# Step sizes of a selective scan from factored quadratics, and low rank experts with spaced gates, in a twelve-sublayer decoder

## Chip, core and metric

The program runs on one NeuronCore of one Trainium2 chip. It is one launch of 31,707 instructions. The metric is the device time of that launch in microseconds (us); of the kernel before three runs were timed.

## What is computed

A decoder of four layers on x of 8 x 128 tokens by 256 features; each layer has an attention-like part, a cross attention and a feed-forward part, and every one of the twelve is followed by a residual addition and a layernorm. The two sublayers that the change touches stand one behind the other, as third and fourth:

```python
def _L0_ffn_ref(x, Wr, br, Wd, bd, Wu, bu):          # E = 8 experts, R = 16, K = 2
    logits = jnp.einsum('btd,de->bte', x, Wr) + br
    gates = jax.nn.softmax(logits + bonus, axis=-1)
    topk_vals, topk_idx = jax.lax.top_k(gates, K)
    topk_vals = topk_vals / topk_vals.sum(axis=-1, keepdims=True)
    w = (jax.nn.one_hot(topk_idx, E, dtype=x.dtype) * topk_vals[..., None]).sum(axis=-2)
    h = jax.nn.relu(jnp.einsum('btd,edr->betr', x, Wd) + bd[None, :, None, :])
    eo = jnp.einsum('betr,erd->betd', h, Wu) + bu[None, :, None, :]
    return jnp.einsum('bte,betd->btd', w, eo)

def _L1_attn_ref(x, W_x, W_dt, b_dt, A_log, D):      # 16 states, rank 64
    dt_x, Bm, Cm = jnp.split(x @ W_x.T, [R, R + N], axis=-1)
    dt = jax.nn.softplus(dt_x @ W_dt.T + b_dt)
    dA = jnp.exp(jnp.einsum('bld,dn->bldn', dt, -jnp.exp(A_log)))
    dBx = jnp.einsum('bld,bln,bld->bldn', dt, Bm, x)
    # h = dA_t * h + dBx_t ; y_t = sum_n h * C_t, over the 128 steps
    return ys.swapaxes(0, 1) + x * D
x = _layernorm(x + _L0_ffn_ref(...)); x = _layernorm(x + _L1_attn_ref(...))
```

## The kernel before

Everything is float32 with tokens of one batch entry on 128 partitions: X is [128, b, 256], its transpose XT [128, c, 1024] with two halves c of the features. Each sublayer is one or more blocks; all engines meet at a block's end, and inside a block each engine runs its own list in the order written, tied to the others by counted semaphores (the names in `p.s`). PSUM has eight banks of 512 columns. The weights of the next sublayer are fetched by SyncE's queue during the present one.

**Low rank experts** (`low_rank_experts`). TensorE computes the router's logits in bank 0 and the hidden values of all experts in banks 1 and 2. VectorE makes the softmax of 8 gates for each token, ranks each gate against the others (L2370 "greater", L2371 "equal", for each of the 8 batch entries, then L2374 to L2376 over all), keeps the two best and scales them (L2380). TensorE turns the gates, eight pieces of 8 columns, into gatesT [8, 1024] (L2336, copied by ScalarE at L2348). VectorE adds the bias to the hidden values and multiplies the rectified ones by their gates (L2384, L2387); TensorE turns them (L2340), ScalarE copies them to hT (L2350).

**The epilogue** (`epilogue`, a helper that most sublayers share). Four rounds j of two batch entries: TensorE writes the sublayer's result for round j into bank j (`products`) and counts up y_ready; VectorE adds it to X (L525), takes statistics (L527, L530) and normalises the even entry (L536 to L539), one round behind; ScalarE does the square root and the odd entry (L504, L509). From round 2 on TensorE also turns the finished X of the round two before (L474) and ScalarE copies it to XT (L414). The experts give epilogue a function y of their own: for each batch entry one product of hT with wu (128 rows, L2392) and one of gatesT with the biases bu (8 rows, L2393), so the two kinds alternate. A float32 product shows as two passes in the trace.

**The selective scan** (`selective_scan`), first block. TensorE projects XT to the rank 64 input of the step sizes (L2574), to B and C (L2578), and the former by w_dt to the raw step sizes in banks 4 to 7 (L2583), then starts the result in banks 0 to 3 (L2591), for which GpSimd prepares selector and read. VectorE splits B and C into three bfloat16 parts (L2617 to L2624). Then it computes dt = softplus(raw + b_dt) = max(v, 0) + u * P(u), with u = exp(-|v|) and P of degree 9 for log(1 + u) / u: the bias (L2627), -|v| (L2766), the exponential by ScalarE (L2760), one scaling and nine Horner steps, each (dt + coefficient) * u, over 128x2048 (L2776, L2778), max and addition (L2779), the product with x (L2630) and a memset in decay (L2632). Each Horner step waits for the one before. The second block is the loop over the 16 states: decays by ScalarE, products by GpSimd, scans and readings by VectorE.

## Time and profile before

| what | us |
|---|---|
| median of three runs (1999.32 to 2001.83) | 1999.76 |
| the profiled execution: device time | 2003.11 |
| its span (first to last instruction) | 2001.3 |
| TensorE busy, with weight loads apart (80% of the span) | 1604.5 |
| VectorE busy (72%) | 1437.1 |
| ScalarE busy (39%) | 777.8 |
| GpSimd busy (26%) | 522.6 |
| low rank experts: first product to the last copy of XT | 731.6 to 776.0 |
| selective scan's first block | 776.3 to 825.2 |
| its loop | 825.5 to 977 |

Busy shares are means over twelve stages with different limits, so they say where an engine works, not where the time is set. The times of the last three lines are positions on the trace's clock. PEclk is the TensorE clock that was granted, as a share of its full 2.4 GHz: 0.50 is 1.2 GHz, and the mean over the span is 0.87. "Idle before" in a row is the time for which the engine did nothing ahead of the instruction; behind the arrow stands what ended it.

### The profile page before, as it was taken

To read this page: it belongs to the slowest core of one execution; us is meant where nothing else is said; L and a number is where in the kernel's file an instruction comes from. 1 tells how busy PE (TensorE), PEld (TensorE's weight loads), DVE (VectorE), ACT (ScalarE), POOL (GpSimd) and SP (SyncE) were. 2 spreads that over 40 slices of the span, in tenths; PEclk is the share of its full clock that TensorE was granted. 3 is DMA by queue.
4 is the path that set the end of the run, shared out by engine and by line. 5 is a ranking of instruction groups with operands and counts; after the bars stand their busy time and mean duration, and the time that the engine had idled before them with its cause. 6 is when DMAs were issued, how large, how long until landed. Compare 5 with 4: busy or idle time off the path is not lost. (4 is left out here: it accounts for less than half of the span.)

```text
span 2001.3 us, 31707 instructions
## 1 busy us (share of the span) xinstructions
PE 1604.5 (80%) x11439; PEld 1193.9 (60%) x11470; DVE 1437.1 (72%) x2398; ACT 777.8 (39%) x1231; POOL 522.6 (26%) x588
## 2 busy tenths in 40 slices
PE   4899999999868987266748568899995997888863
PEld 4678888887854663022446434588774885645631
DVE  3299999998645844899578573556774995657698
ACT  2367777675231532233324321433342002425532
POOL 1233333332412401377213002310000330414200
PEclk8999999999977986587878768999996998798985
DMA  3000000000000000000100001000001220010000
GB/s 143 23 28 29 26 26 26 26 26 1 1 11 13 2 7 34 0 0 0 45 3 2 27 37 72 2 25 11 12 21 42 74 73 27 4 56 2 2 0 21
DMA packets 17854, 49.20 MB, mean 25 GB/s; under 512 B 2003, under 2 KB 8276, under 8 KB 16470
## 3 DMA queue, kind: packets, MB, share of 16 engines
q1 hardware_dynamic: 17750, 47.78, 7.0%
q8 instruction: 69, 1.13, 0.2%
q14 instruction: 35, 0.29, 0.0%
HBM read 46.73 MB, written 1.05 MB: 24 GB/s over the span
## 5 line engine op out<-in xcount | busy, mean ns | idle before, releaser
L2146 DVE SCALAR_TENSOR_TENSOR arena<-psum,arena 128x1016 f32<-128x1016 f32 (+2 forms) x240 | 303.6, 1265 | 35.8 <-ACT arena L2083 30.1
L883 DVE TENSOR_REDUCE limits<-psum 128x4 f32<-128x512 f32 (+2 forms) x256 | 148.3, 620 | 91.9 <-PE psum L743 56.7
L1992 PE MATMUL psum<-ssm_XT_hi,ssm_split 128*128 128x512 f32 x640 | 195.1, 407 | 11.2 <-POOL ssm_split L1951 5.5
L851 ACT ACTIVATE PT<-psum 128x1024 f32<-128x1024 f32 x112 | 108.6, 1022 | 122.2 <-PE psum L774 122.2
L743 PE MATMUL psum<-K,QR 32*128 32x256 f32 (+1 forms) x320 | 125.1, 476 | 27.3 <-POOL K L719 16.5
L1992 PEld LDWEIGHTS psum<-ssm_XT_hi,ssm_split 128*128 128x128 f32 x640 | 116.3, 191 | 36.6 <-POOL ssm_split L1951 10.4
L2083 ACT ACTIVATE arena<-psum,arena 128x1024 f32<-128x1024 f32 x80 | 89.2, 1115 | 106.1 <-PE psum L1992 104.7
L2511 PE MATMUL psum<-expert,x 128*128 128x256 f16 x1024 | 114.2, 276 | 16.6 <-POOL expert L2497 16.6
L2649 POOL TENSOR_TENSOR fed<-dtx,b_all 128x1024 f32<-128x1024 f32 x32 | 103.2, 3245 | 77.8 <-ACT b_all L2698 44.4
L2511 PEld LDWEIGHTS psum<-expert,x 128*128 128x128 f16 x1024 | 101.3, 99 | 29.4 <-issue 16.7
L2524 DVE SCALAR_TENSOR_TENSOR acc<-psum,gate_now,acc 128x256 f32<-128x256 f32 x256 | 111.2, 483 | 8.5 <-PE psum L2511 7.7
L1950 POOL TENSOR_TENSOR ssm_split<-arena,const 128x256 fp32r<-128x256 f32 x80 | 58.5, 731 | 198.7 <-PE psum L1992 196.1
L2718 DVE TENSOR_TENSOR_SCAN state<-decay,fed 128x1024 f32<-128x1024 f32 x32 | 103.1, 3261 | 6.8 <-POOL fed L2649 5.2
L1992 PE MATMUL psum<-ssm_XT_lo,ssm_split 128*128 128x512 f32 x320 | 100.9, 397 | 0.0
L743 PEld LDWEIGHTS psum<-K,QR 32*128 32x128 f32 x320 | 60.8, 219 | 59.3 <-DVE limits L883 22.3
L2662 PE MATMUL psum<-bc_parts,selector 96*128 96x512 bf16 x64 | 23.1, 496 | 86.7 <-DVE read L2726 53.3
L2496 POOL COPY gate_now<-gates 128x8 f32 x32 | 6.1, 191 | 299.5 <-DMA expert_mask<-in_expert_masks 230.8
L762 PE MATMUL psum<-Q,KT 32*128 32x256 f32 (+1 forms) x640 | 82.9, 562 | 0.4
L1305 ACT ACTIVATE probs_g<-psum,negmax_g 128x128 f32<-128x128 f32 x128 | 45.3, 366 | 86.2 <-PE psum L1262 58.8
L498 ACT ACT_TABLE_LOAD x12 | 15.4, 1283 | 156.8 <-PEq L2528 135.3
L625 PE MATMUL psum<-XT,arena 128*128 128x512 f32 x128 | 65.0, 673 | 12.9 <-PEq L911 10.0
L790 PE MATMUL psum<-PT,V 128*32 128x128 f32 x2048 | 73.3, 291 | 2.6 <-DVE O L877 2.6
(435 smaller groups left out, 3828.4 us busy)
## 6 DMA issues: line engine op xcount, KB each, us to landing
expert_mask<-in_expert_masks SPq DMA_DIRECT2D x32, 256.0 KB, 2.6
arena<-in_ssm_in SPq DMA_DIRECT2D x16, 384.0 KB, 2.9
arena<-in_L_xattn SPq DMA_DIRECT2D x1, 5120.0 KB, 16.0
arena<-in_ssm_in SPq DMA_DIRECT2D x16, 256.0 KB, 3.0
arena<-in_L_ffn SPq DMA_DIRECT2D x1, 2592.0 KB, 10.1
arena<-in_L_xattn SPq DMA_DIRECT2D x2, 1280.0 KB, 7.8
arena<-in_L_attn SPq DMA_DIRECT2D x1, 2272.0 KB
arena<-in_L_ffn SPq DMA_DIRECT2D x1, 2176.0 KB, 8.2
```

Of the source, the lines that this page charges most:

```text
L743: ins = nc.tensor.matmul(score_bank(r)[:, k * n:(k + 1) * n], QR[group(r), b % 2, c0 + k, :], K1[group(r), b % 2, c0 + k, :, :].rearrange( ...
L762: nc.tensor.matmul(exponents[r][:, k * n:(k + 1) * n], KT[group(r), c0 + k, b * P:(b + 1) * P], Q1[group(r), b % 2, c0 + k, :, :].rearrang ...
L790: ins = nc.tensor.matmul(raw_bank(k)[group(r), slot * P:(slot + 1) * P], V[:, b, at:at + 32], PT[:, u % 2, r, slot, :], start=True, stop=True)
L851: nc.scalar.activation(PT[:, u % 2, 2 * k:2 * k + 2, :, :].rearrange("p r h q -> p (r h q)"), p.psum[:, (2 + 2 * k) * 512:(4 + 2 * k) * 51 ...
L883: ins = nc.vector.tensor_reduce(limits[:, u % 2, r, :, k], score_bank(r)[:, :].rearrange("p (h k) -> p h k", h=4)[:, :, lo:hi], AX.X, ALU. ...
L1992: ins = nc.tensor.matmul(bank[tile_bank(r, tile) + half][:, :], w_part(tile, kw, c), x_part(kx, c, slice(half * 512, (half + 1) * 512)), s ...
L2083: nc.scalar.activation(conv[:, (r + tile) % 2, :], tile_psum(r, tile), ACT.Copy, scale=tap_now[:, r, tile, TAPS - 1:TAPS]).then_inc(s.tap_ ...
L2146: ins = nc.vector.scalar_tensor_tensor(out[:, :, ago:], product[:, :, :P - ago], tap, out[:, :, ago:], ALU.mult, ALU.add)
L2511: ins = nc.tensor.matmul(bank[b][:, :D], x16[:, part, c, b * P:(b + 1) * P], expert[:, r % 2, c, :], start=(part == 0 and c == 0), stop=(p ...
L2524: nc.vector.scalar_tensor_tensor(acc[:, b, :], bank[b][:, :D], gate[:, r % 2, b:b + 1], acc[:, b, :], ALU.mult, ALU.add).then_inc(s.produc ...
L2649: nc.gpsimd.tensor_tensor(fed[:, c, :], dtx[:, c, :], b_all[:, r, :], ALU.mult).then_inc(s.input_ready.up(trips), 1)
L2718: nc.vector.tensor_tensor_scan(state[:, c, :], decay[:, c, :], fed[:, c, :], 0.0, ALU.mult, ALU.add).then_inc(s.state_ready.up(trips), 1)
```

## The change

In the low rank experts the comparisons are made for all batch entries at once. The scaled gates are also written into `gates_spaced`, [128, 2, 4, 32], where batch entry 2j + k takes the first 8 of 32 columns of group j in half k; GpSimd has cleared the rest. Two transposes then give gatesT [128, 2, 128], in which round j's gates lie on partitions 32j to 32j + 7, and bu is laid out in memory four times, on the same partitions. The function y now fills two rounds at a time: at even j four hidden products (both rounds), the bias products (j, 0), (j+1, 0) and (j, 1); at odd j the last one, (j, 1). Each bias product uses 32 rows of the array, 32j to 32j + 31.

In the scan the polynomial is written as product of four quadratics (u + a)^2 + b and one linear factor. ScalarE computes u = exp(-|raw + b_dt|) from PSUM, the squares, the linear factor and max(raw + b_dt, 0); VectorE multiplies: dt = (square + b) * dt. All of it goes by the two halves c, and two buffers of `factor` for each half let ScalarE run ahead of VectorE. The shifts a are five memsets by GpSimd.

```diff
-                for b in range(B):
-                    ins = nc.tensor.transpose(bank[3 + b // 4][:E, b % 4 * P:(b % 4 + 1) * P], gates[:, b, :], p.c("ident"))
+                for half in range(2):
+                    ins = nc.tensor.transpose(bank[3][:, half * P:(half + 1) * P], spaced[:, half, :, :].rearrange("p j e -> p (j e)"),
+                                              p.c("ident"))
...
-                for b in range(B):
-                    other = gates[:, b, :].rearrange("p (o e) -> p o e", o=1).broadcast_to([P, E, E])
-                    own = gates[:, b, :].rearrange("p (e o) -> p e o", o=1).broadcast_to([P, E, E])
-                    nc.vector.tensor_tensor(above[:, b, :, :], other, own, ALU.is_gt)
-                    ins = nc.vector.tensor_tensor(same[:, b, :, :], other, own, ALU.is_equal)
-                then(ins)
+                other = gates[:, :, :].rearrange("p b (o e) -> p b o e", o=1).broadcast_to([P, B, E, E])
+                own = gates[:, :, :].rearrange("p b (e o) -> p b e o", o=1).broadcast_to([P, B, E, E])
+                nc.vector.tensor_tensor(above[:, :, :, :], other, own, ALU.is_gt)
+                then(nc.vector.tensor_tensor(same[:, :, :, :], other, own, ALU.is_equal))
...
-                nc.vector.tensor_tensor(gates[:, :, :], gates[:, :, :], over_last(small[:, :]), ALU.mult
+                dve.wait_ge(s.operands_ready.sem, s.operands_ready.at(0))
+                pairs = lambda a: a.rearrange("p (j k) e -> p j k e", k=2)
+                nc.vector.tensor_tensor(spaced[:, :, :, :E].rearrange("p k j e -> p j k e"), pairs(gates[:, :, :]), pairs(over_last(small[:, :])), ALU.mult
                                         ).then_inc(s.gates_ready.up(), 1)
+                then(nc.vector.tensor_tensor(gates[:, :, :], gates[:, :, :], over_last(small[:, :]), ALU.mult))
...
-        def y(b, dst):
-            nc.tensor.matmul(dst, hT[:, b, :], p.w("wu"), start=True, stop=False)
-            return nc.tensor.matmul(dst, gatesT[:, b * P:(b + 1) * P], p.w("bu")[:E, :], start=False, stop=True)
+        def y(j, bank):
+            def hidden(j, k):
+                nc.tensor.matmul(bank[j][:, k * D:(k + 1) * D], hT[:, 2 * j + k, :], p.w("wu"), start=(k == 0), stop=False)
+
+            def biases(j, k):
+                group = slice(32 * j, 32 * j + 32)
+                return nc.tensor.matmul(bank[j][:, k * D:(k + 1) * D], gatesT[group, k, :], p.w("bu")[group, :], start=False, stop=(k == 1))
+
+            if j % 2:
+                return biases(j, 1)
+            for n in range(4):
+                hidden(j + n // 2, n % 2)
+            biases(j, 0)
+            biases(j + 1, 0)
+            return biases(j, 1)
...
             @block.gpsimd
             def _(pool):
+                for k, v in enumerate([a for a, _ in quadratics] + [offset]):
+                    ins = nc.gpsimd.memset(shifts[:, k:k + 1], v)
+                ins.then_inc(s.terms_ready.up(), 1)
...
-                softplus_act(p, act, state[:, :, :])
-                nc.scalar.preload_act_table(ACT.Exp)
+                act.wait_ge(s.tile_ready.sem, s.tile_ready.at(2))
+                act.wait_ge(s.terms_ready.sem, s.terms_ready.at(0))
+                raw = lambda c: p.psum[:, (4 + 2 * c) * 512:(6 + 2 * c) * 512]
+
+                def next_factor(c, k):
+                    if k >= 2:
+                        act.wait_ge(s.term_product.sem, s.term_product.at(2 * (k - 2) + c))
+                    dst, shift = factor[:, c, k % 2, :], shifts[:, k:k + 1]
+                    if k < Q:
+                        ins = nc.scalar.activation(dst, state[:, c, :], ACT.Square, bias=shift)
+                    else:
+                        ins = nc.scalar.activation(dst, state[:, c, :], ACT.Identity, scale=slope, bias=shift)
+                    ins.then_inc(s.factor_ready.up(), 1)
+
+                for c in range(DC):
+                    then(nc.scalar.activation(state[:, c, :], raw(c), ACT.Abs, bias=p.w("b_dt")[:, c:c + 1]))
+                    then(nc.scalar.activation(state[:, c, :], state[:, c, :], ACT.Exp, scale=-1.0))
+                    next_factor(c, 0)
+                for k in range(1, Q + 1):
+                    for c in range(DC):
+                        next_factor(c, k)
+                    if k == 2:
+                        for c in range(DC):
+                            nc.scalar.activation(xy[:, c, :], raw(c), ACT.Relu, bias=p.w("b_dt")[:, c:c + 1]).then_inc(s.relu_ready.up(), 1)
...
-                dve.wait_ge(s.tile_ready.sem, s.tile_ready.at(2))
+                for k in range(Q + 1):
+                    for c in range(DC):
+                        dve.wait_ge(s.factor_ready.sem, s.factor_ready.at(DC * k + c))
+                        if k:
+                            dve.wait_ge(s.term_product.sem, s.term_product.at(DC * (k - 1) + c))
+                        by = state[:, c, :] if k == 0 else dt[:, c, :]
+                        if k < Q:
+                            ins = nc.vector.scalar_tensor_tensor(dt[:, c, :], factor[:, c, k % 2, :], quadratics[k][1], by, ALU.add, ALU.mult)
+                        else:
+                            ins = nc.vector.tensor_tensor(dt[:, c, :], factor[:, c, k % 2, :], by, ALU.mult)
+                        ins.then_inc(s.term_product.up(), 1)
                 for c in range(DC):
-                    ins = nc.vector.tensor_scalar(xy[:, c, :], p.psum[:, (4 + 2 * c) * 512:(6 + 2 * c) * 512], p.w("b_dt")[:, c:c + 1], None, ALU.add)
-                then(ins)
-                softplus_dve(p, dve, dt[:, :, :], xy[:, :, :], state[:, :, :])
-                then(nc.vector.tensor_tensor(dtx[:, :, :], dt[:, :, :], p.XT[:, :, :], ALU.mult))
+                    dve.wait_ge(s.relu_ready.sem, s.relu_ready.at(c))
+                    dve.wait_ge(s.term_product.sem, s.term_product.at(DC * Q + c))
+                    then(nc.vector.tensor_tensor(dt[:, c, :], dt[:, c, :], xy[:, c, :], ALU.add))
+                    nc.vector.tensor_tensor(dtx[:, c, :], dt[:, c, :], p.XT[:, c, :], ALU.mult)
```

`quadratics` holds the four pairs (a, b) from the complex roots of the fitted polynomial, Q is 4, and the fifth factor comes from its one real root, with the leading coefficient in it.

Three places, by the order of instructions on one engine. First TensorE in the experts' epilogue, before (hT_experts are the hidden products, gatesT the biases; X are transposes):

```order
L2392 MATMUL psum<-arena,hT_experts 128x256
L2393 MATMUL psum<-arena,gatesT 128x256
L2392 MATMUL psum<-arena,hT_experts 128x256
L2393 MATMUL psum<-arena,gatesT 128x256
L2392 MATMUL psum<-arena,hT_experts 128x256
L2393 MATMUL psum<-arena,gatesT 128x256
L474 MATMUL psum<-const,X 128x128 x4
L2392 MATMUL psum<-arena,hT_experts 128x256
L2393 MATMUL psum<-arena,gatesT 128x256
L2392 MATMUL psum<-arena,hT_experts 128x256
L2393 MATMUL psum<-arena,gatesT 128x256
L474 MATMUL psum<-const,X 128x128 x12
```

and after the change, from the block's first product on:

```order
L2403 MATMUL psum<-arena,hT_experts 128x256 x4
L2407 MATMUL psum<-arena,gatesT 128x256 x4
L2403 MATMUL psum<-arena,hT_experts 128x256 x4
L2407 MATMUL psum<-arena,gatesT 128x256 x3
L478 MATMUL psum<-const,X 128x128 x4
L2407 MATMUL psum<-arena,gatesT 128x256
L478 MATMUL psum<-const,X 128x128 x12
```

The alternation of hidden and bias products becomes runs of four, and of the second run of biases the last one, that of j = 3, stands behind the first transposes.

Second, ScalarE in the first block of the scan, before:

```order
L2605 COPY dt_in<-psum 64x1024
L2606 ACT_TABLE_LOAD
L2606 ACTIVATE a<-arena 128x32
L2607 ACTIVATE a<-a 128x32
L2760 ACTIVATE state<-state 128x2048
L2609 ACT_TABLE_LOAD
```

and now:

```order
L2634 COPY dt_in<-psum 64x1024
L2635 ACT_TABLE_LOAD
L2635 ACTIVATE a<-arena 128x32
L2636 ACTIVATE a<-a 128x32
L2652 ACTIVATE state<-psum,arena 128x1024
L2653 ACTIVATE state<-state 128x1024
L2646 ACTIVATE factor<-state,shifts 128x1024
L2652 ACTIVATE state<-psum,arena 128x1024
L2653 ACTIVATE state<-state 128x1024
L2646 ACTIVATE factor<-state,shifts 128x1024 x5
L2660 ACTIVATE xy<-psum,arena 128x1024 x2
L2646 ACTIVATE factor<-state,shifts 128x1024 x2
L2648 ACTIVATE factor<-state,shifts 128x1024 x2
```

One exponential over 128x2048 and a second table load were there; now sixteen operations on 128x1024, Abs at L2652, Exp at L2653, Square at L2646, Relu at L2660 and the linear factor at L2648, behind one table load.

Third, VectorE in the same block from the last part of B and C on, before:

```order
L2624 CAST bc_parts<-bc_rest 32x1024
L2627 TENSOR_SCALAR xy<-psum,arena 128x1024 x2
L2766 SCALAR_TENSOR_TENSOR state<-xy 128x2048
L2776 TENSOR_SCALAR dt<-state 128x2048
L2778 SCALAR_TENSOR_TENSOR dt<-dt,state 128x2048 x9
L2779 SCALAR_TENSOR_TENSOR dt<-xy,dt 128x2048
L2630 TENSOR_TENSOR dtx<-dt,XT 128x2048
L2632 MEMSET decay 128x16
```

and now:

```order
L2675 CAST bc_parts<-bc_rest 32x1024
L2683 SCALAR_TENSOR_TENSOR dt<-factor,state 128x1024 x2
L2683 SCALAR_TENSOR_TENSOR dt<-factor,dt 128x1024 x6
L2685 TENSOR_TENSOR dt<-factor,dt 128x1024 x2
L2690 TENSOR_TENSOR dt<-dt,xy 128x1024
L2691 TENSOR_TENSOR dtx<-dt,XT 128x1024
L2690 TENSOR_TENSOR dt<-dt,xy 128x1024
L2691 TENSOR_TENSOR dtx<-dt,XT 128x1024
L2693 MEMSET decay 128x16
```

The bias, -|v|, the scaling and the Horner steps on full width are gone from VectorE; ten products, two additions and two products with x on half the width stand there.

## Rows read from the trace of the kernel before

**Rows 1.** Table of stretches: us, busy PE, PEld, DVE, ACT, POOL, then PEclk, DMA share, GB/s

```profile
751.70:776.20 24.50, 22.20 (x48) 10.86 (x48) 8.93 (x32) 6.72 (x13) 0.00 (x0) 0.50 0.00 0
...
791.40:825.20 33.80, 1.13 (x3) 0.19 (x1) 31.26 (x16) 3.19 (x2) 0.00 (x0) 0.58 0.00 0
825.20:977.00 151.80, 96.80 (x200) 38.03 (x200) 138.99 (x64) 52.45 (x48) 103.17 (x32) 0.80 0.00 0
```

**Rows 2.** Timeline before the scan loop: start, length, engine, line, operation, [idle before <-releaser]

```profile
779.85 3.60 POOL L2598 TENSOR_TENSOR read<-XT,arena 128x2048 f32<-128x2048 f32 x1
...
785.20 3.70 PE L2583 MATMUL psum<-dt_in,arena 64*128 64x512 f32 x8
...
791.38 2.48 DVE L2627 TENSOR_SCALAR xy<-psum,arena 128x1024 f32<-128x1024 f32 x2
...
796.28 1.91 ACT L2760 ACTIVATE state<-state 128x2048 f32<-128x2048 f32 x1 [11.77 <-DVE state L2766]
...
798.23 1.23 DVE L2776 TENSOR_SCALAR dt<-state 128x2048 f32<-128x2048 f32 x1 [2.04 <-ACT state L2760]
799.49 20.90 DVE L2778 SCALAR_TENSOR_TENSOR dt<-dt,state 128x2048 f32<-128x2048 f32 x9
...
825.12 0.07 DVE L2632 MEMSET decay<- 128x16 f32 x1
```

**Rows 3.** Groups by shape (busy, mean ns), then two back-to-back pairs of the timeline

```profile
L953 ACT ACTIVATE cos<-turns,tiny 128x1024 f32<-128x1024 f32 x1 | 1.1, 1133 | 0.0
L952 ACT ACTIVATE sin<-angle 128x1024 f32<-128x1024 f32 x1 | 1.1, 1057 | 11.6 <-DVE turns L946 11.6
...
827.59 2.18 ACT L2703 ACTIVATE decay<-dt,a 128x1016 f32<-128x1016 f32 x2
...
508.68 2.36 DVE L2230 TENSOR_TENSOR ssm_scaled<-ssm_gated,arena 128x1024 f32<-128x1024 f32 x2
```

**Rows 4.** Timeline of the gates in the low rank experts

```profile
740.62 0.23 DVE L2370 TENSOR_TENSOR above<-gates 128x64 f32<-128x64 f32 x1
...
742.91 0.69 DVE L2374 TENSOR_TENSOR same<-same,const 128x512 f32<-128x512 f32 x1
...
746.17 1.23 DVE L2384 TENSOR_TENSOR h_experts<-psum,arena 128x1024 f32<-128x1024 f32 x1
...
748.71 1.66 PE L2340 MATMUL psum<-const,h_experts 128*128 128x128 f32 x8 [1.56 <-DVE h_experts L2387]
```

**Rows 5.** Timeline of the epilogue after them

```profile
751.77 1.19 PE L2392 MATMUL psum<-arena,hT_experts 128*128 128x256 f32 x2 [1.40 <-PEq L2317]
...
765.53 1.11 PE L474 MATMUL psum<-const,X 128*128 128x128 f32 x4
...
770.99 0.69 DVE L525 TENSOR_TENSOR added<-X,psum 128x512 f32<-128x512 f32 x1 [3.02 <-PE psum L2393]
...
775.38 0.59 ACT L414 COPY XT<-psum 128x512 f32<-128x512 f32 x1 [0.27 <-PE psum L474]
```

**Rows 6.** TensorE: dense products at 0.50, their stretches, and four row groups

```profile
716.31 2.26 PE L466 MATMUL psum<-arena,OT 128*128 128x256 f32 x5
...
717.59 0.98 PE L466 MATMUL psum<-arena,OT 128*128 128x256 f32 x2
...
715.80:718.20 2.40, 2.40 (x7) 0.50 0.00 0
719.20:720.80 1.60, 1.60 (x11) 1.00 0.00 0
...
1229.75 2.09 PE L762 MATMUL psum<-Q,KT 32*128 32x256 f32 x16
```

**Rows 7.** Timeline: VectorE's additions in the epilogue of the attention before

```profile
721.28 0.69 DVE L525 TENSOR_TENSOR added<-X,psum 128x512 f32<-128x512 f32 x1 [0.41 <-PE psum L466]
...
723.53 0.68 DVE L525 TENSOR_TENSOR added<-X,psum 128x512 f32<-128x512 f32 x1
```

**Rows 8.** Timeline: the first projection of the scan

```profile
776.31 5.35 PE L2574 MATMUL psum<-XT,arena 128*64 128x512 f32 x8 [0.97 <-PEq L423]
```

46 lines of the change are left out of this document (26 added, 20 removed).

## The prediction

> **What bounds the kernel now.** I read three views. The table of stretches shows which engine fills which piece of time: in the 33.8 us before the scan loop VectorE is busy 31.26 us, ScalarE 3.19 and TensorE 1.13, so this stretch is a VectorE chain with two idle neighbours; in the 24.5 us of the low rank experts' epilogue TensorE is busy 22.20 us at a granted clock of 0.50 and VectorE 8.93 [rows 1]. The timeline then gives the order inside both [rows 2 to 5]. The chain of waits on the page ends in the last layernorm and says nothing of either place, and the whole-span shares (PE 80%, DVE 72%) mix stages, so neither is used. Both places are serial pieces of a program in which every sublayer waits for the one before: what they lose in length comes off the span, unless something else is late there.
>
> **The scan's step sizes: what stands there.** VectorE starts the softplus at 791.38 and writes the last value, the memset, at 825.12: 33.7 us. In it nine Horner steps on 128x2048 take 20.90 us [rows 2]. ScalarE takes part with one exponential. TensorE delivered the raw step sizes well before, at about 788.9 (the products start at 785.20 and last 3.70), and VectorE picks them up late because its work on B and C ends at 791.4.
>
> **What stands there after.** The degree 9 polynomial (ten coefficients) becomes four quadratics and a linear factor. ScalarE makes Abs, Exp and five factors for each half of 128x1024, and two Relu: 2 x (1+1+5) + 2 = 16 operations. VectorE keeps ten products and, per half, one addition and the product with x. Price of a ScalarE step: 1.13 us alone with a bias from memory, 1.06 without; issued back to back the pair of decays takes 2.18 for two, so the second adds 2.18 - 1.13 = 1.05 [rows 3]. Price of a VectorE step: 1.23 alone, as L2384 on the same shape [rows 4]; a pair takes 2.36, so a following one adds 1.14 [rows 3]. Abs, Relu, Square and Identity at this shape are not in the trace. I take the price of the sine at L953, since all share form and bias; the bounds are 0.96 below, the exponential's 1.91 for two halves, and 1.24 above, VectorE's 2.48 for two halves read from PSUM at L2627 [rows 2].
>
> ScalarE starts at 789.0, 2.4 us before VectorE did, because it is idle since the scaling of a. Abs 1.13, wait for itself 0.04, Exp 1.06, wait 0.04, factor 1.05: 3.32 for a half, 6.6 for both; then eight factors and two Relu at 1.05 are 10.5. The last factor ends at 789.0 + 6.6 + 10.5 = 806.1. VectorE is the faster of the two per step only where it needn't wait: its ten products (11.4 us) follow the factors and cannot end earlier. So ScalarE sets the pace, and VectorE adds a tail: last product 1.23 (the other half's addition goes behind it at 1.14), the product with x behind its addition 1.26, addition of the second half 1.14, its product with x 1.26, less what the first overlaps: 806.2, 807.3, 808.6, 809.7, 811.0 are the five starts, and the memset starts at 812.2. Against 825.12 that is **12.9 us less**. B and C's work stays on VectorE up to 791.4 and hides: the first factor is done at 792.4. The five small memsets on GpSimd delay selector and read by five small operations; TensorE needs them at 788.8, and read ends at 783.45 [rows 2], so they cost nothing. The loop waits for the block's end and doesn't see which engine was last. The program order has one table load here, not two; the one dropped ran beside VectorE and gives nothing back.
>
> **The experts' gates.** Sixteen comparisons of 128x64 fill 740.62 to 742.91, 2.29 us; the two of 128x512 cost 0.69 each, like L2374, overlap by some 0.08 and wait 0.04: 1.33 [rows 4]. That is 0.96 less. A second scaling of the gates (one issue, 0.14) now stands between the spaced gates and the addition at L2384: **0.8 us less** up to the start of the products. The transposes fall from eight to two and the copy to ScalarE shrinks, but both lie beside VectorE's two steps on h_experts, from 746.17 until TensorE turns the result at 748.71 [rows 4]: nothing.
>
> **The products.** Now hidden and bias products alternate; from 751.77 to the transposes at 765.53 are twelve, 1.147 us each [rows 5]. The same shape without a change of row count runs at 0.50 with passes 2.26 - 0.98 = 1.28 us for three, 0.427 apart, so 0.853 per product of two passes [rows 6]. The difference, 0.3 us, is the price of each change between 128 rows and 8. After: four hidden products (3.41), a change (0.3), then biases of j, j+1, j in two row groups. Sixteen passes on four row groups took 2.09 us, where one behind the other they would take 6.8 at 0.427, and 3.4 at the full clock [rows 6]; so different groups do run side by side. In my case group j has four passes in a row, 1.71, and group j+1 runs beside it. Counted from the first product: y 0 ready at 5.4, y 1 at 5.9, the next four hidden to 9.8, y 2 at 11.5, four transposes and the last bias with two changes to y 3 at 13.8. VectorE wants 2.25 us for each j (from 721.28 to 723.53) [rows 7], so it takes y 2 at 11.6 and y 3 at 13.9. Behind it comes the tail of before, from 770.99 to 775.97: 4.98 [rows 5]. End at 18.9, where it was 775.97 - 751.77 = 24.2: **5.3 us less**. It moves y 0 later (5.4 for 4 x 1.147 = 4.6) and the later ones earlier; the first delay is eaten by the wait for y 2.
>
> **Sum.** 12.9 + 0.8 + 5.3 = 19.0. The profiled execution took 2003.11 with a span of 2001.3, so it would be 1984.1 and 1982.3; the median of three lies 3.35 lower, and the forecast against it is 1999.76 - 19.0 = 1980.8.
>
> **Rivals.** First, **the clock rises in the epilogue**. Before, 24.5 us at 0.50 with TensorE almost always occupied, but in passes with gaps at each change [rows 1, 5]; in the epilogue of the attention before, dense products of 128 rows go from 0.50 to 1.00 after some 3 us [rows 6]. After the change there are two dense runs of 3.4 us. If the clock rises during the second, y 2 comes 1.2 us earlier and the last transposes end 0.7 earlier: 1978.9. The same could shorten the first projection of the scan (5.35 for eight passes, of which four at half speed [rows 8]) or lengthen it by some 1.7. The Trainium skill, page TensorE: Matmul & The Clock Gate, section What's actually happening, says that sustained activity releases the throttle; this stretch, busy on paper throughout and at 0.50, speaks against taking occupancy for activity, and by the rule as it reads the sum would be 21 instead of 19.
>
> Second, **the two row groups don't overlap**, since each product has two passes and both bias products of a group lie close. Then each bias product takes its own 0.853, y 0 is at 6.3, y 2 at 13.7, y 3 at 16.0, the end at 21.0: 3.2 instead of 5.3, 1982.9. The rows for four groups speak against it.
>
> Third, **ScalarE's steps or the hand-offs cost more**: 1.24 instead of 1.05, with another 0.1 of waiting behind each of sixteen steps, is 4.6 us, 1985.4; at the lower bound of 0.96 it would be 1.4 us faster, 1979.4. Hand-offs of the trace speak against (ScalarE's exponential ends at 798.19, VectorE goes on at 798.23) [rows 2].
>
> Fourth, on the other side: **ScalarE becomes a bound worse than VectorE was**. The chain has 16 steps; the change is slower than before when each costs 19.0 / 16 = 1.2 us more, 2.3 in place of 1.1, as with a squaring or an absolute value that runs at half rate. At 2.6 the time would be 1999.76 - 19.0 + 16 x 1.5 = 2004.8. Against it: two sines, an exponential and a pair of decays on ScalarE all lie from 0.96 to 1.13 us for 128x1024, under VectorE's 1.23 [rows 2 to 4]. The Trainium skill, page ScalarE: Activation LUTs, section Rules for kernel authors, speaks for this side: it wants relu, add and mul on VectorE, which it calls up to three times faster in bf16. By such a ratio to VectorE's 1.23 the sixteen steps would cost an estimated 59 us and the change would lose 23. The rows, in float32, have no such ratio.
>
> The scan loop behind it is VectorE's, 138.99 of 151.8 us [rows 1], and nothing in it is edited, so its clock isn't a rival. But all later stages start 19 us earlier against the clock's rises and falls, for which I allow 2 us either way.
>
> **How the numbers follow.** As reckoned, 0.52: 1980.8. Clock rises, 0.20: 1978.9. No overlap of groups, 0.12: 1982.9. Dearer steps, 0.12: up to 1985.4. Nearly all given back later, 0.02: within 0.2%. ScalarE the bound, 0.02: 2004.8. The range for 8 in 10 runs from 1976.5 (clock case less its 2 us) to 1985.5 (no overlap plus 2). 0.2% is 4 us, about what can be told from no change here; faster 0.96, same 0.02, slower 0.02.
>
> **What would show it.** Memset of decay some 12.9 us earlier relative to the end of the w_dt products; ScalarE without idle from Abs to the last factor, steps 1.05 apart; VectorE waiting for ScalarE before each product; bias passes of two groups starting within 0.1 us; y 2 about 11.5 us after the first product; 2.25 us between the last two additions. A gap in ScalarE before the third factor, or a Square above 1.2 us, would break the first term; a stretch at 1.00 would break the second towards faster.

## The result and the profile after

The changed kernel takes 1982.04 us (median of four runs, 1976.48 to 1984.11), and the kernel before takes 2000.8 beside it (1999.32 to 2003.15). The ratio is 0.9901 with a 95% interval of 0.9876 to 0.9925: of 2000.8 that is 19.8 us saved, somewhere between 15 and 25, where the two medians are 18.8 apart. The prediction, 1980.8, lies 1.2 us below, and the time lies in its range of 1976.5 to 1985.5. The profiled execution is the one of 1984.11, with a span of 1982.3.

The first view is the table of stretches. Its columns are the stretch, its length, the busy time of TensorE, its weight loads, VectorE, ScalarE and GpSimd with their counts, the granted clock, the DMA share and GB/s. The first three lines are the experts' epilogue, whose counterpart is the first line of [rows 1].

```profile
748.14:757.20 9.06, 9.06 (x24) 6.20 (x24) 3.13 (x10) 1.54 (x2) 0.00 (x0) 0.50 0.01 2
757.20:760.60 3.40, 2.52 (x13) 1.38 (x12) 2.61 (x13) 1.10 (x4) 0.00 (x0) 1.00 0.00 0
760.60:765.76 5.16, 3.08 (x12) 2.10 (x12) 2.96 (x12) 3.97 (x9) 0.00 (x0) 0.50 0.00 2
...
774.96:803.09 28.13, 7.96 (x19) 2.89 (x17) 22.25 (x22) 16.84 (x16) 0.00 (x0) 0.73 0.00 0
803.09:952.00 148.91, 88.97 (x191) 35.28 (x192) 139.02 (x64) 52.42 (x48) 103.13 (x32) 0.83 0.00 0
```

TensorE's granted clock in the epilogue was 0.50 from end to end, the lower of its two levels (1.2 GHz). Now it rises to 1.00 (2.4 GHz) for the 3.4 us in the middle. Before the loop ScalarE has come in beside VectorE: 16.84 us of work where it had 3.19. The loop holds the same work as before, VectorE 139.02 against 138.99.

The second view is the timeline before the scan loop (start, length, engine, line, operation, and in brackets the idle time before it and who ended it), which answers to [rows 2].

```profile
775.59 3.70 PE L2609 MATMUL psum<-dt_in,arena 64*128 64x512 f32 x8
...
779.38 1.11 ACT L2652 ACTIVATE state<-psum,arena 128x1024 f32<-128x1024 f32 x1 [4.48 <-PE psum L2609]
780.53 1.06 ACT L2653 ACTIVATE state<-state 128x1024 f32<-128x1024 f32 x1
...
784.89 5.31 ACT L2646 ACTIVATE factor<-state,shifts 128x1024 f32<-128x1024 f32 x5
...
786.07 1.22 DVE L2683 SCALAR_TENSOR_TENSOR dt<-factor,state 128x1024 f32<-128x1024 f32 x1 [2.04 <-ACT factor L2646]
787.21 4.62 DVE L2683 SCALAR_TENSOR_TENSOR dt<-factor,dt 128x1024 f32<-128x1024 f32 x4
...
790.10 2.09 ACT L2660 ACTIVATE xy<-psum,arena 128x1024 f32<-128x1024 f32 x2
...
793.27 2.36 DVE L2683 SCALAR_TENSOR_TENSOR dt<-factor,dt 128x1024 f32<-128x1024 f32 x2 [1.43 <-ACT factor L2646]
...
794.18 2.18 ACT L2648 ACTIVATE factor<-state,shifts 128x1024 f32<-128x1024 f32 x2
...
802.65 0.07 DVE L2693 MEMSET decay<- 128x16 f32 x1
```

ScalarE goes from 779.38 to 796.36 without a pause, and every idle time in VectorE's rows is ended by a factor of ScalarE. From the start of the w_dt products to the memset it is 802.65 - 775.59 = 27.06, where it was 825.12 - 785.20 = 39.92 [rows 2]. (The table below has 27.05, from unrounded times.)

The third view is the timeline of the gates, the epilogue and the first projection, for [rows 4, 5, 8].

```profile
738.47 0.69 DVE L2379 TENSOR_TENSOR above<-gates 128x512 f32<-128x512 f32 x1
739.07 0.68 DVE L2380 TENSOR_TENSOR same<-gates 128x512 f32<-128x512 f32 x1
739.79 0.69 DVE L2382 TENSOR_TENSOR same<-same,const 128x512 f32<-128x512 f32 x1
...
745.65 1.09 PE L2350 MATMUL psum<-const,h_experts 128*128 128x128 f32 x8 [2.21 <-DVE h_experts L2397]
748.14 3.75 PE L2403 MATMUL psum<-arena,hT_experts 128*128 128x256 f32 x8 [1.40 <-PEq L2322]
751.83 2.08 PE L2407 MATMUL psum<-arena,gatesT 32*128 32x256 f32 x8
753.83 3.62 PE L2403 MATMUL psum<-arena,hT_experts 128*128 128x256 f32 x8
...
753.93 0.69 DVE L529 TENSOR_TENSOR added<-X,psum 128x512 f32<-128x512 f32 x1 [8.34 <-PE psum L2407]
...
757.38 1.13 PE L2407 MATMUL psum<-arena,gatesT 32*128 32x256 f32 x6
...
758.55 0.69 DVE L529 TENSOR_TENSOR added<-X,psum 128x512 f32<-128x512 f32 x1 [0.65 <-PE psum L2407]
...
760.79 0.68 DVE L529 TENSOR_TENSOR added<-X,psum 128x512 f32<-128x512 f32 x1
...
765.17 0.59 ACT L419 COPY XT<-psum 128x512 f32<-128x512 f32 x1 [0.27 <-PE psum L478]
...
766.10 5.96 PE L2600 MATMUL psum<-XT,arena 128*64 128x512 f32 x8 [0.97 <-PEq L428]
```

The epilogue lasts from 748.14 to the end of the last copy at 765.76, 17.62 us, where it was 24.2. Eight passes of bias products start at 751.83 and the next product at 753.83: 2.00 us for eight at 0.50, a quarter of a microsecond each against 0.427 for dense passes one behind the other [rows 6]. These eight go in pairs, one pass on each row group, with starts at most 0.01 us apart.

Every difference between the two profiled executions, up to the last square root of the last layernorm (its deviation), by sections that begin and end with the same operation, in us. Each layernorm is marked by the last of its square roots:

| Section | before | after | difference |
|---|---|---|---|
| start to the second sublayer's layernorm | 728.04 | 725.89 | -2.15 |
| router, gates, up to the addition at h_experts | 18.13 | 17.23 | -0.90 |
| from there to the first product of y | 5.60 | 5.03 | -0.57 |
| epilogue, to the last copy | 24.20 | 17.62 | -6.58 |
| last copy to the w_dt products | 9.23 | 9.83 | +0.60 |
| w_dt products to the memset | 39.92 | 27.05 | -12.87 |
| memset to the last reading of the loop | 144.69 | 144.67 | -0.02 |
| last reading to the next layernorm | 17.88 | 20.79 | +2.91 |
| everything behind | 1009.44 | 1009.74 | +0.30 |
| sum | 1997.13 | 1977.85 | -19.28 |

The five sections from the gates to the memset, the only ones that are edited or border on an edit, save 20.3 us. The sections that nothing touches differ by 1.0 in all, but that hides -2.15 and +2.91. The second of them is one of the questions below. (Where an experiment below gives the section from the first product to the third layernorm's marker, that is the epilogue without its last 3.2 us: 21.01 before, 14.43 after.)

### The profile page after: what moved, and what is told of

It is laid out like the page before. It is cut to its first block and busy times, and to the rows that moved or that the text cites. A ratio compares the mean times of both kernels' runs of the same rounds, so it can differ in the third digit from the quotient of the medians.

```text
span 1982.3 us, 31716 instructions
## 1 busy us (share of the span) xinstructions
PE 1594.9 (80%) x11433; PEld 1193.6 (60%) x11464; DVE 1416.8 (71%) x2384; ACT 790.5 (40%) x1245; POOL 522.6 (26%) x594
## 3 DMA queue, kind: packets, MB, share of 16 engines
q8 instruction: 69, 1.13, 0.2%
HBM read 46.73 MB, written 1.05 MB: 24 GB/s over the span
## 5 line engine op out<-in xcount | busy, mean ns | idle before, releaser
L629 PE MATMUL psum<-XT,arena 128*128 128x512 f32 x128 | 65.1, 673 | 12.9 <-PEq L915 10.0
```

## The experiments

Two questions were open. First, how much of the epilogue's gain is what the prediction said, order and overlap at a clock of 0.50, and how much its first rival, a clock that rises? And is it the packing on row groups that lets it rise, or the place in time? Second, are the 2.9 us at the loop's end a price of the change, a gain that is given back, or the clock's own? Beside them stood the two theories of the scan's first term: ScalarE's chain, or VectorE's steps. The time of each section is that of the one profiled execution; intervals are those of the ratios against the kernel before on the same chip.

### The whole change again, twice

Both are the changed kernel without an edit, each beside its own runs of the kernel before.

> The whole change once more, beside the parts of it on the same chip. Theory (the prediction's sum): 19 us less than before. In the first profile the length from the last reading of the scan loop to the last square root of the layernorm behind it was 20.8 us where before had 17.9, with TensorE's last additions and transposes at 0.50. If this belongs to the clock's rises and falls and not to the change, it can come out as 17.9 or as 20.8 in this profile, and the total spreads by as much; if it belongs to the change, it is 20.8 again in every profile that has it.

Measured: 1982.55 us (1980.0 to 1985.45), ratio 0.9904 [0.9887, 0.992].

> The changed kernel once more, unedited, as the base for the three runs beside it on the same chip. My theory and its rival give the same: 1980 to 1985 us; from the end of the w_dt transposes to the memset of the last decay 27.05 us; from the last reading of the scan loop to the next sublayer's first marker 17.6 or 20.8, by where the granted clock stands.

Measured: 1983.17 us (1980.9 to 1986.52), ratio 0.9909 [0.9893, 0.9926]. In both w_dt to memset is 27.06, gates and epilogue are within 0.05 us of the first trace, and the clock rises for 3.4 us in the middle of the epilogue. The result holds on three occasions. From the last reading to the next layernorm both show 20.79 again; what that says is told under the loop's end.

### Each part alone

With the scan's part alone, the kernel before has the new softplus:

```diff
-                softplus_act(p, act, state[:, :, :])
-                nc.scalar.preload_act_table(ACT.Exp)
...
+                for k in range(1, Q + 1):
+                    for c in range(DC):
+                        next_factor(c, k)
```

> Only the scan's step sizes are changed, the low rank experts are as before. Theory (ScalarE sets the pace with sixteen steps): 12.9 us less from the start of the w_dt products to the memset of decay, so 27.0 us there where before had 39.9, and 1987 to 1989 us in all against 2000.8. Rival (part of it is given back at the end of the loop because the clock is lower there): the same 27.0 us, but only some 10 us less in all.

Measured: 1990.5 us (1987.05 to 1991.96), ratio 0.9942 [0.9925, 0.9958]; the median lies above the 1987 to 1989 that were expected. w_dt to memset is 27.06 as in the whole change; gates and epilogue are those of before, with the clock at 0.50 from end to end:

```profile
750.60:775.00 24.40, 22.20 (x48) 10.86 (x48) 8.90 (x32) 6.55 (x14) 0.00 (x0) 0.50 0.00 1
```

With the experts' part alone, the changed kernel has the old softplus:

```diff
+                softplus_act(p, act, state[:, :, :])
+                nc.scalar.preload_act_table(ACT.Exp)
...
-                for k in range(1, Q + 1):
-                    for c in range(DC):
-                        next_factor(c, k)
```

> Only the low rank experts are changed, the scan is as before. Theory (runs of hidden products, biases on four row groups, comparisons all at once): the epilogue from its first product to the last copy of XT takes 17.0 to 18.9 us where before had 24.2, depending on whether the clock rises in it, the gates 0.8 less, and the whole 6 to 8 us less than before. Rival (it lives from the scan part or from a lucky clock): less than 4 us.

Measured: 1989.01 us (1988.0 to 1992.55), ratio 0.9934 [0.9917, 0.995]. w_dt to memset is 39.91. The epilogue, first product to the last copy, takes 15.62 us, below the 17.0 to 18.9 that were expected, and the whole saves more than the expected 6 to 8. The clock rises some 6 us sooner after the first product than in the whole change, and first product to the layernorm's marker is 12.43 for 14.43. The timeline of TensorE there, then two stretches of it (length, TensorE's busy time, granted clock, DMA share, GB/s):

```profile
749.13 3.44 PE L2403 MATMUL psum<-arena,hT_experts 128*128 128x256 f32 x8 [1.40 <-PEq L2322]
752.50 1.13 PE L2407 MATMUL psum<-arena,gatesT 32*128 32x256 f32 x8
753.56 1.99 PE L2403 MATMUL psum<-arena,hT_experts 128*128 128x256 f32 x8
755.49 1.13 PE L2407 MATMUL psum<-arena,gatesT 32*128 32x256 f32 x6
```

```profile
749.10:752.10 3.00, 2.97 (x7) 0.50 0.03 5
752.15:758.90 6.75, 5.68 (x30) 1.00 0.00 0
```

The clock is up at 752.15, before the first bias pass at 752.50: here the packed products can't be what raised it.

Eight passes on two row groups take 1.06 us here at 1.00 and 2.00 at 0.50. The parts save 11.4 and 12.9 us against 19.3 for the whole in these runs, so their sum is 5 us too large. With intervals of some 3 us on each, and 2 us of it in the epilogue's clock, that is no proof of an interaction. By the sections there is none: what is edited has the same length alone and together.

### The bias products on one row group

The order of the changed kernel stays, but eight transposes again lay all gates on partitions 0 to 7 of gatesT, and each bias product reads 8 rows of one group, as before:

```diff
-                group = slice(32 * j, 32 * j + 32)
-                return nc.tensor.matmul(bank[j][:, k * D:(k + 1) * D], gatesT[group, k, :], p.w("bu")[group, :], start=False, stop=(k == 1))
+                b = 2 * j + k
+                return nc.tensor.matmul(bank[j][:, k * D:(k + 1) * D], gatesT[:, b * P:(b + 1) * P], p.w("bu")[:E, :], start=False, stop=(k == 1))
```

> The whole change, but the bias products use eight rows of the first row group again, with gatesT of 8 x 1024 as before; the new order of products (four hidden, then the biases) stays. Theory A (bias products of two row groups run side by side): without that each of eight bias products takes 0.85 us at 0.50 of its own, so the seven-pass-pair runs of biases last 3.4 us at 0.50 where the change has 2.1, and the epilogue takes 1.5 to 2.5 us longer than with the change (19 to 20 in place of 17.6). Theory B (only the fewer changes between 128 rows and few rows count): the same 17.6 us as with the change.

> The same kernel as in the earlier run with the bias products on 8 rows of one group, in the new order. If it is the packing on four row groups that lets the clock rise in the experts' epilogue, the granted clock stays at 0.50 here from the first product to the last transposes, and first product to the third layernorm's marker is 18.1 us again. If the rise is a matter of where this stretch happens to fall in time, it may rise here too, after some 9 to 10 us, and the stretch takes 15 to 17 us.

Measured: 1984.74 us (1981.84 to 1986.66), ratio 0.9917 [0.9901, 0.9934]; in the second run 1986.81, 0.9933 [0.9908, 0.9958]. First the timeline of the first of them, then the stretch from its first product to beyond the epilogue, and the same stretch of the second:

```profile
748.93 3.75 PE L2402 MATMUL psum<-arena,hT_experts 128*128 128x256 f32 x8 [1.40 <-PEq L2322]
752.62 3.78 PE L2406 MATMUL psum<-arena,gatesT 8*128 8x256 f32 x8
756.33 3.78 PE L2402 MATMUL psum<-arena,hT_experts 128*128 128x256 f32 x8
760.04 2.92 PE L2406 MATMUL psum<-arena,gatesT 8*128 8x256 f32 x6
```

```profile
748.90:774.90 26.00, 23.65 (x54) 13.95 (x55) 8.70 (x32) 6.64 (x13) 4.39 (x7) 0.50 0.13 46
```

```profile
748.80:774.80 26.00, 23.68 (x54) 13.92 (x55) 8.70 (x32) 6.61 (x13) 4.42 (x7) 0.50 0.13 45
```

Three things follow. The order alone, without packing, takes the section from the first product to the marker from 21.01 to 18.09, 2.9 us, against 3.2 by the second rival's sum. Eight bias passes in one group take 756.33 - 752.62 = 3.71, and on two groups 2.00: the groups overlap. And the clock stays at 0.50 although TensorE is busy for 23.65 of 26.00 us. Packing is worth another 18.09 - 14.43 = 3.7 us, more than the 1.5 to 2.5 that were expected of it. The passes tell how it divides, as an estimate: 1.7 in the first run of biases (3.71 for 2.00), and 0.8 in the second, which takes 2.92 in one group and would take 2.08 packed at 0.50, since its group j has four passes as in the first run. That is 2.6 for the overlap at an unchanged clock. The other 1.1 is the clock: the second run of biases takes 1.13 and not 2.08, and the hidden products ahead of it are 0.15 shorter.

### Packing or place in time

One more trace of the kernel before was taken, unedited.

> The kernel before, unedited, once more with a profile: does the granted clock stay at 0.50 through the experts' epilogue, as in its first trace? If packing is what lets it rise, yes: first product to the last copy 24.2 us. If the phase does, it may rise here.

Measured: one run of 1997.35 us. Here the clock falls three products into the epilogue, at 749.9, and does not rise again until 773.8; the section is 19.29 us where it was 21.01. The first rows of its timeline, passes at 1.00 and then at 0.50:

```profile
747.87 0.67 PE L2392 MATMUL psum<-arena,hT_experts 128*128 128x256 f32 x2 [1.40 <-PEq L2317]
...
751.86 1.22 PE L2393 MATMUL psum<-arena,gatesT 8*128 8x256 f32 x2
```

So the place in time moves where the clock falls, and gives or takes up to 2 us; this trace's 22.47 us to the last copy is not the 24.2 that was expected if packing decides, though the clock did stay down once it had fallen.

The traces fall into groups by where the clock fell before or behind the epilogue's first product, and where it rose next (us from the first product; the first bias pass starts at 3.3 to 3.7 in the new order):

| traces | bias products | fell | rose |
|---|---|---|---|
| changed kernel three times, rectifications on VectorE, linear factor first | packed | -1.1 to -1.2 | 9.0 to 9.1 |
| one row group, twice | 8 rows | -1.2 | 26.1 |
| experts' part alone, both with a fill at the loop's end (below) | packed | -0.4 to -0.6 | 2.9 to 3.0 |
| the kernel before, scan's part alone | 8 rows | -2.6 to -2.7 | 28.0 to 28.1 |
| the kernel before again | 8 rows | 2.1 | 26.0 |

The first two lines are the comparison that counts: the clock falls at the same place, the first products run alike, and only the packed kernel gets the rise at 9.0, in five traces against two. That is 0.2 us before its second run of packed products, so if packing brought it about, it was by the first run or by what came sooner for it. In the third group the rise comes before any packed pass, and no 8-row trace fell at that place, so there it isn't shown what let the clock rise. All eight packed traces had a rise before the first projection and none of the five others had, but packing is shown as the difference only where the clock fell some 1.2 us ahead of the first product. Which quality of it counts, the denser passes, the rows of the array that they use or the earlier start of the products behind them, was not tried.

### The rectifications on VectorE

```diff
-                    if k == 2:
-                        for c in range(DC):
-                            nc.scalar.activation(xy[:, c, :], raw(c), ACT.Relu, bias=p.w("b_dt")[:, c:c + 1]).then_inc(s.relu_ready.up(), 1)
...
+                        if k == 0:
+                            dve.wait_ge(p.act_chain.sem, abs_done[c])
+                            nc.vector.tensor_scalar(xy[:, c, :], p.psum[:, (4 + 2 * c) * 512:(6 + 2 * c) * 512], p.w("b_dt")[:, c:c + 1], 0.0,
+                                                    ALU.add, ALU.max).then_inc(s.relu_ready.up(), 1)
```

> The two rectifications max(raw + b, 0) are made by VectorE before its first product, in time in which it waits for ScalarE anyway, and not by ScalarE. If ScalarE's chain sets the pace of the scan's step sizes, as my sum had it, its chain gets two steps of 1.05 shorter less what VectorE's last products can't follow: w_dt to memset falls from 27.05 us to 25.6 +- 0.4. The rival, that VectorE's own 14 steps with their hand-offs set the length, makes it 1 to 2 us longer: 28 to 29.5. The time would be 1.4 less or 1 to 2 more than the unedited kernel's, beside up to 3 us of clock at the loop's end.

Measured: 1983.07 us (1980.19 to 1984.56), ratio 0.991 [0.9893, 0.9926], so the whole time doesn't tell it from the changed kernel's 0.9909. The section does: 25.54 for 27.05, within the 25.6 +- 0.4 that was expected. VectorE's timeline shows the new step in the time that it used to wait, and a wait that has shrunk from 2.04 to 0.69:

```profile
784.26 1.28 DVE L2679 TENSOR_SCALAR xy<-psum,arena 128x1024 f32<-128x1024 f32 x1
...
788.56 1.23 DVE L2686 SCALAR_TENSOR_TENSOR dt<-factor,state 128x1024 f32<-128x1024 f32 x1 [0.69 <-ACT factor L2647]
```

VectorE has two steps more and the section is 1.5 us shorter: ScalarE's chain is what sets it. The rival, VectorE's own steps, would have made it longer.

### The linear factor first, by VectorE

```diff
-                    if k < Q:
-                        ins = nc.scalar.activation(dst, state[:, c, :], ACT.Square, bias=shift)
-                    else:
-                        ins = nc.scalar.activation(dst, state[:, c, :], ACT.Identity, scale=slope, bias=shift)
+                    nc.scalar.activation(factor[:, c, k % 2, :], state[:, c, :], ACT.Square, scale=by_root if k == 0 else 1.0,
+                                         bias=shifts[:, k:k + 1]).then_inc(s.factor_ready.up(), 1)
...
+                        if k == 0:
+                            dve.wait_ge(p.act_chain.sem, exp_done[c])
+                            nc.vector.scalar_tensor_tensor(dt[:, c, :], state[:, c, :], -root, state[:, c, :], ALU.add, ALU.mult
+                                                           ).then_inc(s.term_product.up(), 1)
```

> The linear factor of the polynomial is no longer made by ScalarE: VectorE makes (u - root) u from u in one step, at once when u is there, while ScalarE squares; the sign goes into the last step, the scale into the first square. ScalarE has 14 steps in place of 16, VectorE 14 as before. If ScalarE's chain sets the pace: w_dt to memset 23.3 us +- 0.7 in place of 27.05 (two steps of 1.05 less, and VectorE's tail starts with one product fewer behind the last square), total about 3.7 below the unedited kernel's. If VectorE's own steps did: unchanged, 27 +- 0.5.

Measured: 1978.12 us (1970.43 to 1979.45), ratio 0.9876 [0.9851, 0.9902]; w_dt to memset 23.42. Its timeline:

```profile
786.02 7.39 ACT L2646 ACTIVATE factor<-state,shifts 128x1024 f32<-128x1024 f32 x7
793.32 2.09 ACT L2658 ACTIVATE xy<-psum,arena 128x1024 f32<-128x1024 f32 x2
...
786.02 1.22 DVE L2678 SCALAR_TENSOR_TENSOR dt<-state 128x1024 f32<-128x1024 f32 x1 [0.56 <-ACT state L2651]
787.35 8.04 DVE L2682 SCALAR_TENSOR_TENSOR dt<-factor,dt 128x1024 f32<-128x1024 f32 x7
795.31 1.22 DVE L2687 TENSOR_TENSOR dt<-xy,dt 128x1024 f32<-128x1024 f32 x1
```

With 14 steps for 16 on ScalarE the section loses 3.6 us, as ScalarE's chain would have it (23.3 +- 0.7 expected). From 786.02 on VectorE runs to the end without a wait, so there its own steps, 1.14 apart, now set the length; ScalarE's last factor is done only 0.8 us before VectorE takes it up, so to gain much more both would have to get shorter. At 1978.1 against 1983.2 for the changed kernel on the same chip this is the lowest median of the study, though the two intervals overlap a little, and the two kernels with a fill (below) are not told from it.

### The loop's end

What TensorE does behind the last reading, in the changed kernel and in the run with the linear factor first:

```profile
947.45 5.40 PE L2731 MATMUL psum<-read,const 128*128 128x512 f32 x8 [3.62 <-DVE read L2787]
...
958.53 3.60 PE L2797 MATMUL psum<-const,xy 128*128 128x128 f32 x16 [2.25 <-PEq L2696]
```

```profile
944.99 3.70 PE L2728 MATMUL psum<-read,const 128*128 128x512 f32 x8 [1.02 <-DVE read L2784]
...
954.37 1.94 PE L2794 MATMUL psum<-const,xy 128*128 128x128 f32 x16 [2.25 <-PEq L2693]
```

The same eight additions take 5.40 or 3.70, the same sixteen transposes 3.60 or 1.94, by the clock. From the last reading to the next layernorm it is 17.88 and 21.07 in the two traces of before, 20.79 in three of the changed kernel, 20.71 with the experts' part alone, 19.29 with the scan's alone, 18.99 with the rectifications on VectorE, 17.59 and 17.60 with one row group, 17.59 with the linear factor first. So 2.9 us is no fixed price of the change, since the kernel before has 21.07 in its second trace; against that one the change gains 0.3 there. But the changed kernel had the long one in all three traces, as was expected if it belonged to the change, and the short one only with an edit that moves its place in time. Two traces of before are too few to say how often it gets which, so a price of some fraction of the 2.9 isn't ruled out. One run tried to steer the clock there, by twelve products of zeros in TensorE's idle time:

```diff
+                for n in range(WARM):
+                    nc.tensor.matmul(bank[n % 4][:, :], p.c16("ident"), zeros[:, :], start=False, stop=False)
                 add(NS - 1, 1, 1)
```

> Twelve bf16 matmuls of zeros with 512 columns are added where TensorE waits about 3.6 us for the last reading of the scan loop, so that it goes into the last additions without a pause. Theory: the pause, or where it falls, decides whether the last additions and transposes run at 1.00 (3.70 and 1.94 us) or 0.50 (5.40 and 3.60); filled, last reading to the next sublayer is 17.6 to 17.9 us. Rival: the granted clock there doesn't depend on what TensorE did just before; it stays at 20.8 in as many runs as before, or the zeros themselves run at 0.50 (12 x 0.43 = 5.1 us) and delay the additions by about 1.5 us: 22.

> Both edits on top of the changed kernel: the linear factor made first by VectorE, and the twelve matmuls of zeros before the last additions of the scan loop. If the two savings are independent, w_dt to memset is 23.4 us, as in the run with the factor alone, and the last additions take 3.6 us and not 5.4. Against the unedited changed kernel (0.9909 of before on the second chip call) 3.6 + 1.7 = 5.3 us, so a ratio of 0.988 and 1976 to 1978 us. The rival, that a clock bought in one place is taken back in the next one (in the run with the fill alone the transposes behind the additions then ran at 0.50 and took 3.36 us), leaves 3.6 to 4 us: 1978 to 1979.

Measured: with the fill alone 1979.26 us (1977.16 to 1981.44), ratio 0.9897 [0.9881, 0.9914]; with the linear factor as well 1978.18 (1976.61 to 1980.71), 0.9892 [0.9873, 0.9911], no better than the linear factor alone and above the 1976 to 1978 expected of two independent savings; w_dt to memset is 23.42. The timeline of the fill alone:

```profile
942.75 2.75 PE L2749 MATMUL psum<-zeros_scan,const 128*128 128x512 bf16 x12
945.34 3.60 PE L2734 MATMUL psum<-read,const 128*128 128x512 f32 x8
...
954.62 3.36 PE L2802 MATMUL psum<-const,xy 128*128 128x128 f32 x16 [2.25 <-PEq L2699]
```

The additions run at 1.00, and the transposes behind a wait of 2.25 us at 0.50. But the zeros didn't bring that about. A stretch of the same trace (length, TensorE's busy time, granted clock, DMA share, GB/s) has the clock up from 941.20 on, 1.5 us before the first zero:

```profile
941.20:954.80 13.60, 11.35 (x34) 1.00 0.00 0
```

In four traces without a fill (before, one row group twice, linear factor first) the clock rose at the same place, 2.3 to 2.6 us ahead of the last reading, where the two with zeros have 2.6 and 2.8. The additions ran at 1.00 in those four as well. In them the transposes did too, and the section is 17.6 to 17.9; with the zeros it is 19.91 in both runs. The zeros still run when the last reading is done, the additions and the transposes start some 1.1 us later for it, and the clock falls before the transposes. So against traces with the clock in the same place the fill costs some 2 us, and the 17.6 to 17.9 of the theory was missed. The 19.91 is 0.9 less than the changed kernel's 20.79, where the clock stood otherwise. The lower total of the run with the fill alone is not told from the changed kernel's, since the intervals overlap, and its trace has other short parts that lie far ahead of the zeros, such as 2 us in the experts' epilogue.

## Why the prediction came out right

**The scan's step sizes: 12.9 predicted, 12.87 measured.** Each step of the sum holds. ScalarE starts 3.79 us behind the first w_dt product (predicted 3.8). Its steps last 1.06 to 1.15 and follow one another at 1.00 to 1.05; the last factor ends 16.98 us after the start (predicted 17.1), and the memset stands 23.27 after the start (predicted 23.2). The price taken from the sine of [rows 3], an operation of another function with the same form, was that of Abs, Square, Identity and Relu alike: neither the dearer steps of the third rival nor the slow ones of the fourth came. What the text had not foreseen is small: the two Relu in the middle leave VectorE waiting 1.43 us there, and the run without them shows that they cost 1.5. The rule that the prediction quoted from the Trainium skill, page ScalarE: Activation LUTs, section Rules for kernel authors, wants such steps on VectorE. For float32 the traces show no such ratio, 1.05 against 1.14 us back to back. Yet where VectorE waits anyway, moving two steps over did pay.

**The gates: 0.8 predicted, 0.90 measured.** The two comparisons take 739.79 - 738.47 = 1.32 (predicted 1.33), and the section ahead of them is equally long in both traces. No run changed the gates alone. The section behind them is 0.57 shorter for another reason, which the sum put at nothing: eight transposes took 1.66 us in the first trace at the lower clock [rows 4] and 1.09 now. In the second trace of before they took 1.09 as well, so this is the clock's and not the change's.

**The epilogue: 5.3 predicted, 6.6 measured.** The step that failed is the assumption that the clock stays at 0.50; the first rival, given 0.20, is what happened in part. y 2 is taken up at 758.55 - 748.14 = 10.4 (the sum said 11.6, the rival 1.2 less). The clock rises at 9.0, at the end of the second run of hidden products; with the first run's 2.08 in place of 1.13 and 0.15 more for the hidden products y 2 would be ready at 11.5, which is the sum's figure. The rival's other 0.7, for the last transposes, did not come: the clock is back at 0.50 by then and the last eight take 1.97 as before. So the epilogue gained 1.3 over the sum and not 1.9. The 11.5 also holds two errors that cancel: the sum let group j + 1 end 0.5 behind group j, where the two end together and the next products start 0.4 sooner, and it took four passes in a row for 1.71, where the first run shows 2.08 with the slower pass behind the change of rows and the whole length of the last one. The same 2.08 is why y 0 is taken up at 5.8 for 5.4. The last two additions are 2.24 apart (predicted 2.25). The tail from the last addition is 4.97 (predicted 4.98).

The runs with one row group, with TensorE 23.65 us busy of 26.00 and never above 0.50, show that a TensorE that is busy in the profile isn't enough to raise its clock. The Trainium skill, page TensorE: Matmul & The Clock Gate, section What's actually happening, has the throttle released by sustained activity. The rule as it reads made the sum 21, and the edited sections measured 20.3; these two runs don't bear it out if activity is read as busy time.

**What the sum left out.** The first projection is 5.96 for 5.35, since the clock rises 4.7 us after its start where it was 3.5: +0.6, inside the "lengthen it by some 1.7" of the first rival. And the allowance of 2 us for the later stages' clock was too narrow for a single execution, which showed 2.9 in one place, but wide enough for the median. Over all thirteen traces the part before the second sublayer's layernorm, which nothing edits, lasts 725.5 to 728.4 us, and the part behind the scan's layernorm 1006.3 to 1010.5. The range, too, is a little wider than its own words: 1978.9 less 2 is 1976.9 and 1982.9 plus 2 is 1984.9; nothing hangs on it here.

So the median came out at 1982.04 for 1980.8 although the edited sections saved 20.3 rather than 19.0. The saving by medians is known to some 5 us either way, and the two numbers don't contradict each other. That the forecast lies as near as 1.2 us to the median is in part luck: the scan's term is right by mechanism and size, but the epilogue's was too small by 1.3, and stretches that nothing edits moved by -2.15 and +2.91 in the two traces.

## What to carry to other kernels

When a serial polynomial sits on one engine, writing it as a product of factors turns it into a pipeline over two engines, and, while the other engine still waits, the new length is read from the one that makes the factors: count its steps, price them from a row of the same shape and form, and add the other engine's tail. Then look where the second engine still waits; here one factor made first by VectorE was worth 3.6 us more. And compare sections that end in the same operation rather than whole spans, since untouched stretches differ by 3 to 4 us from trace to trace, the stretch at the loop's end by the clock alone. And before a change in the clock is put down to an edit, look whether it comes before or behind the edited instructions, and compare traces in which the clock fell at the same place.

## What the runs showed of the hardware

- With TensorE 23.65 us busy of 26.00 the clock stayed at 0.50. Where it had fallen some 1.2 us ahead of the epilogue's first product, it rose 9.0 us behind it in all five traces with bias products packed on row groups, and not within 26 us in the two with 8 rows in one group. In three other packed traces it rose before the first packed pass.
- Float32 passes of 32 rows and 256 columns on two row groups run in pairs: eight take 2.00 us at 0.50 and 1.06 us at 1.00, up to the start of the next product, against 3.71 at 0.50 in one group.
- The same stretch at the loop's end lasts from 17.6 to 21.1 us by where the clock stands in it. Twelve bf16 products of zeros there didn't raise the clock, which was up 1.5 us before them, and the stretch was 2 us longer than in the four traces without them that had the clock rise at the same place.
- ScalarE's Abs, Square, Identity, Relu and Exp on 128x1024 float32 last nearly the same, 1.06 to 1.16 us, from PSUM or from SBUF, and follow one another at 1.00 to 1.05.
